# A four-layer graph network: attention over 626 node columns in place of 640, and another division of labour in the one-hot preparation

## The chip, the core and the metric

The kernel runs on one core of a Trainium2 chip. A core has a matrix engine (TensorE, PE in the profile), a vector engine (VectorE, DVE), an activation engine (ScalarE, ACT), GpSimd (POOL) and a queue for transfers (SyncE, SP). The first four compute side by side and wait for one another by semaphores; each works through its own queue in order. The metric is the time of one execution on the device, in microseconds (us).

## What is computed

Node features `x` [625, 512] go through four graph layers, each behind a layer norm and a relu, each added to `x`. There are 20,000 edges, sorted by destination.

```
h = relu(layernorm(x)); x = x + relu(mean over incoming h[src] @ W_l.T + b_l + h @ W_r.T)   # layer 0
h = relu(layernorm(x)); x = x + transformer(h)                                               # layer 1
h = relu(layernorm(x)); x = x + (sum of w(e) h[row], scaled by degrees) @ lin_w.T + lin_b    # layer 2
   w(e) = sigmoid(edge_attr_3 @ conf_w.T + conf_b)
h = relu(layernorm(x)); x = x + edge network with 64 attributes per edge                     # layer 3
# layer 1, 4 blocks: y = conditioned norm; scores = q[src] . k[dst] per head (4 heads of 128),
#   softmax over the edges of each src, out = sum of attn * v[dst]; then an MLP of 512
```

## The kernel before

Nodes lie in five tiles of 128, so 625 nodes take NP = 640 columns, and a half is HALF = 320. The program has three stages of its own: `front`, `transformer_and_gcn`, `edge_layer`; only the first two are touched.

**front** turns the edge list into two dense matrices between nodes: the count of edges, and their sum of weights. The edges are taken in 40 groups of 512 (4 tiles of 128 edges). For each tile `from_onehot` [128 edges, 640] marks the source and `to_onehot` [128 edges, 3, 64] marks the destination within a window of 64 nodes, once plain and twice multiplied by the weight's high and low part `wb`. A product on PE adds a group to PSUM, and DVE adds every second group's result into `sums` [128, 5, 3, 704], which has to be zero before. The work is divided so:

- SP loads the rows, destinations and sources first, then the attributes.
- GpSimd writes the iota (L337) and the identity (L338, L340); in the loop it multiplies `to_onehot` by the weights (L350, `weighted`).
- ScalarE fills `sums` with zeros, five instructions of 2112 elements per partition (L362), with the Exp of the weights' argument `wz` between the third and the fourth (L361). In the loop it makes the last tile of each `from_onehot` (L371, L374).
- VectorE converts the indices (L548 to L561), computes `wz` (L563 to L565), finds the windows from the rows (L569 to L581; `windows_known` lets all the engines into the loop), makes the weights (L584 to L591: plus one, reciprocal, clamp and scale, high part, back, difference, low part). Then it compares sources for groups 0 and 1 (`compare_from`, L608, three instructions per group), destinations for 0 to 3 (`compare_to`, L600), sources for 2 and 3, waits for `sums_zero`, and enters the loop. A ring of four buffers holds the groups; in the loop DVE waits for PE's group and refills.

**transformer_and_gcn** runs the four blocks. Weights and activations of the large products are split in a high and a low part, three products for one (`three`, L989). Per block: v, then q and k by feature (4 features x 2 parts, FIRST = 384 columns and REST = 256), then the attention over 20 score tiles (4 heads x 5 tiles of 128 queries). In step n PE makes the score tile n (L1068, two halves of 320 keys), turns tile n - 2 (L1076, five transposes of 128), and, from n = 8 on, makes parts of the output product of an earlier head (L1089). DVE adds the logarithm of the edge counts and takes the maximum in one instruction (L1446), ACT takes the exponential with the sum (L1267), DVE takes the reciprocal (L1453) and scales (L1456), ACT evicts the turned tile (L1273). The output is split by ACT (L1280) and DVE (L1384). A score or output product in full fp32 shows as two records each in the profile. At the head of this stage DVE takes the moments of the last tile and splits `cw` (L1392), for which PE's first product (L1017) waits. `Plan` gives each product its PSUM bank and its number on a semaphore. GpSimd splits `cw` for the coming block in mid-attention (L962) and adds row biases (L973). The second layer's matrices and the third layer use the semaphores `gcn_wt` and `gcn_lb` for their loads.

## Time and profile before

| | us |
|---|---|
| median of 3 runs | 1647.14 (1646.83 to 1648.19) |
| the profiled execution, its own time | 1645.13 |
| its span, first to last instruction | 1643.5 |
| TensorE busy | 1557.3 (95%) |
| VectorE busy | 1189.6 (72%) |
| ScalarE busy | 1102.0 (67%) |
| GpSimd busy | 677.4 (41%) |
| TensorE clock granted, mean | 0.992 |

Busy time is an average over stages. `front` takes about the first 177 us, the transformer and the second graph layer run to about 860 us, and the edge layer from there to the end. A timeline row has its start, its length, and in brackets the idle time of the engine before it, with what ended it. Short instructions on one engine can overlap by a part of their length, so starts, not lengths, tell the pace. The records of TensorE overlap too.

### The profile page before, as it was taken

To read this page: it belongs to the slowest core of one execution; us is meant where nothing else is said; L and a number is where in the kernel's file an instruction comes from. 1 tells how busy PE (TensorE), PEld (TensorE's weight loads), DVE (VectorE), ACT (ScalarE), POOL (GpSimd) and SP (SyncE) were. 2 spreads that over 40 slices of the span, in tenths; PEclk is the share of its full clock that TensorE was granted. 3 is DMA by queue.
4 is the path that set the end of the run, shared out by engine and by line. 5 is a ranking of instruction groups with operands and counts; after the bars stand their busy time and mean duration, and the time that the engine had idled before them with its cause. 6 is when DMAs were issued, how large, how long until landed. Compare 5 with 4: busy or idle time off the path is not lost. (4 is left out here: it accounts for less than half of the span.)

```text
span 1643.5 us, 24989 instructions
## 1 busy us (share of the span) xinstructions
PE 1557.3 (95%) x8530; PEld 1218.5 (74%) x8530; DVE 1189.6 (72%) x1896; ACT 1102.0 (67%) x1534; POOL 677.4 (41%) x498
## 2 busy tenths in 40 slices
PE   5889899999999999999999999999999999999987
PEld 4765586888788778877854777777777777777874
DVE  8977656556465646475723599888898888889877
ACT  9841545544554546454530699999999999999963
POOL 3410200120012001200302788788888888888601
PEclk9999899999999999999999999999999999999989
DMA  3001320012012200212007867777777777777710
GB/s 106 0 20 66 96 78 27 28 58 87 22 33 84 77 1 33 84 33 90 28 3 232 160 142 151 144 149 147 145 150 145 150 147 148 146 148 149 172 39 32
DMA packets 107046, 153.94 MB, mean 94 GB/s; under 512 B 42042, under 2 KB 47034, under 8 KB 106466
## 3 DMA queue, kind: packets, MB, share of 16 engines
q0 software_dynamic: 72832, 87.84, 28.1%
q1 hardware_dynamic: 34146, 65.21, 12.5%
q8 instruction: 41, 0.67, 0.2%
q14 instruction: 27, 0.22, 0.0%
HBM read 141.02 MB, written 11.73 MB: 93 GB/s over the span
## 5 line engine op out<-in xcount | busy, mean ns | idle before, releaser
L1772 POOL DMA_INDIRECT edge_gathered<-dst_table,edge_index x158 | 266.4, 1686 | 58.7 <-issue 53.6
L223 PE MATMUL edge_z2p<-edge_w_hi,edge_h_hi 128*128 128x512 f32 x628 | 256.6, 409 | 1.7 <-DVE edge_late L2095 1.7
L223 PE MATMUL edge_z2p<-edge_w_hi,edge_h_lo 128*128 128x512 f32 x628 | 248.6, 396 | 0.0
L223 PE MATMUL edge_z2p<-edge_w_lo,edge_h_hi 128*128 128x512 f32 x628 | 248.3, 395 | 0.0
L1741 POOL DMA_INDIRECT edge_gathered<-src_table,edge_index x158 | 201.6, 1276 | 85.4 <-POOL edge_index L1735 30.6
L973 POOL TENSOR_TENSOR h<-h,tr_row_b 128x512 f32<-128x512 f32 x40 | 59.2, 1513 | 274.2 <-ACT C L1213 273.8
L962 POOL TENSOR_TENSOR tr_cw<-w_c,tr_cw 32x1024 fp32r<-32x1024 f32 x7 | 16.6, 2376 | 346.1 <-ACT tr_cw L1173 346.1
L223 PEld LDWEIGHTS edge_z2p<-edge_w_hi,edge_h_hi 128*128 128x128 f32 x628 | 117.9, 188 | 54.9 <-issue 29.8
L223 PEld LDWEIGHTS edge_z2p<-edge_w_hi,edge_h_lo 128*128 128x128 f32 x628 | 118.1, 188 | 28.7
L223 PEld LDWEIGHTS edge_z2p<-edge_w_lo,edge_h_hi 128*128 128x128 f32 x628 | 118.1, 188 | 24.7
L2095 DVE TENSOR_TENSOR edge_late<-edge_z2p,w_c 128x1024 f32<-128x1024 f32 x79 | 96.7, 1224 | 44.9 <-PE edge_z2p L223 44.6
L989 PE MATMUL tr_one<-tr_yT_hi,tr_w_hi 128*128 128x256 f32 (+1 forms) x384 | 118.8, 309 | 4.3 <-issue 4.3
L989 PE MATMUL tr_one<-tr_yT_hi,tr_w_lo 128*128 128x256 f32 (+1 forms) x384 | 117.8, 307 | 0.0
L989 PE MATMUL tr_one<-tr_yT_lo,tr_w_hi 128*128 128x256 f32 (+1 forms) x384 | 117.8, 307 | 0.0
L2112 DVE SCALAR_TENSOR_TENSOR edge_early<-edge_early,edge_z1p 128x1024 f32<-128x1024 f32 x79 | 96.1, 1217 | 27.8 <-ACT edge_early L1981 27.8
L1267 ACT ACTIVATE hT<-hT,tr_nmax 128x640 f32<-128x640 f32 x56 | 46.3, 828 | 95.8 <-DVE tr_nmax L1446 95.4
L1977 ACT ACTIVATE edge_early<-edge_early 128x1024 f32<-128x1024 f32 x79 | 83.9, 1062 | 27.1 <-DVE edge_early L2069 27.0
L1068 PE MATMUL tr_two<-tr_kT,tr_qT 128*128 128x320 f32 x320 | 99.9, 439 | 0.1
L2123 DVE TENSOR_TENSOR edge_h_lo<-edge_early,edge_h_hi 128x1024 fp32r<-128x1024 f32 x79 | 96.8, 1225 | 2.7
L2076 DVE SCALAR_TENSOR_TENSOR edge_late<-edge_late 128x1024 f32<-128x1024 f32 x79 | 95.8, 1212 | 0.3 <-ACT edge_late L1990 0.3
L1446 DVE CUSTOM_DVE_ANT_0 hT<-tr_two,logc 128x640 f32<-128x640 f32 x80 | 65.8, 822 | 37.0 <-PE tr_two L1068 35.7
L1987 ACT ACTIVATE edge_late<-edge_late 128x1024 f32<-128x1024 f32 x79 | 82.8, 1048 | 9.6 <-DVE edge_late L2095 8.1
(364 smaller groups left out, 4019.9 us busy)
## 6 DMA issues: line engine op xcount, KB each, us to landing
w_c<-in_attr_T SPq DMA_DIRECT2D x78, 128.0 KB, 4.1
agg<-edge_sum_rows POOLq DMA_DIRECT2D x36, 128.0 KB, 10.6
w_a<-in_wv SPq DMA_DIRECT2D x4, 1024.0 KB, 5.3
w_b<-in_wq SPq DMA_DIRECT2D x4, 1024.0 KB, 5.5
w_a<-in_wk SPq DMA_DIRECT2D x4, 1024.0 KB, 7.8
w_b<-in_wo SPq DMA_DIRECT2D x4, 1024.0 KB, 7.1
w_a<-in_m SPq DMA_DIRECT2D x4, 1024.0 KB, 5.4
w_b<-in_m SPq DMA_DIRECT2D x4, 1024.0 KB, 5.3
```

The costliest lines, as they stand in the source:

```text
L223: mm = pe.matmul(out, a, b, start=(n == 0), stop=(n == last))
L989: mm = pe.matmul(out, a, b, start=(start and n == 0), stop=(stop and n == len(terms) - 1))
L1068: mm = pe.matmul(bank[:, f, 0:HALF], qT[:, h, i * P:(i + 1) * P], kT[:, h, f * HALF:(f + 1) * HALF], start=True, stop=True)
L1446: ins = dve.tensor_tensor_reduce(out=cols(scores[n % 2], HALF), in0=bank[:, :, 0:HALF], in1=cols(k.logc[:, i, :], HALF), scale=-1.0, scala ...
L1741: pool.indirect_dma_start(out=from_rows[a][:, j, :].bitcast(F32), out_offset=None, in_=k.src_table, in_offset=bass.IndirectOffsetOnAxis(ap ...
L1772: pool.indirect_dma_start(out=from_rows[ring][:, j, :].bitcast(F32), out_offset=None, in_=k.dst_table, in_offset=bass.IndirectOffsetOnAxis ...
L1977: act.activation(m1[one], m1[one], ACT.Square).then_inc(S["inner1_ready"], 1)
L1987: act.activation(m2[two], z2[two], ACT.Exp).then_inc(S["e2_ready"], 1)
L2076: dve.scalar_tensor_tensor(h2[new], m2[new], 0.5, z2[new], ALU.subtract, ALU.mult).then_inc(S["h2_ready"], 1)
L2095: dve.tensor_tensor(cols(z2[two], D), cols(ps_z2[:, :], D), b2[:, None, :].to_broadcast([P, PT, D]), ALU.add).then_inc(S["z2_ready"], 1)
L2112: dve.scalar_tensor_tensor(m1[one], m1[one], 0.5, ps_z1[one][:, :], ALU.subtract, ALU.mult).then_inc(S["h1_ready"], 1)
L2123: dve.tensor_tensor(h1_lo[one][:, :, :], cols(m1[one], EDGE), h1_hi[one][:, :, :].bitcast(F32), ALU.subtract).then_inc(S["lo_ready"], 1)
```

## The change

Attention: queries stay 5 tiles of 128, but keys and output columns end at USED = 626, in two parts of PART_A = 313. The products for q and k take 370 and 256 columns (QK_HALVES) in place of 384 and 256; the MLP keeps 384 and 256. L1446, the exponential, the scaling and the split of the output work on 626 or 313 columns. The last tile of an output product has 114 rows. Columns 626 to 640 of `qT` and of `probs_more` are filled with zeros once, by DVE at the head of the stage, and PE waits for that ahead of its first score tile. Transposes and their evictions keep 640 columns.

Preparation: GpSimd fills `sums` in place of ScalarE. ScalarE takes the Exp, and makes the reciprocal as Ln and Exp and the high part as a copy. VectorE keeps the addition of one (with a limit of 1e18 ahead of it), which now stands before the windows' table, and two instructions for the low part. Destinations are compared first. Two pairs of load semaphores become one each.

```diff
+LARGE = 1.0e18
...
@@ block.gpsimd, front @@
+                for i in range(NT):
+                    pool.memset(sums[:, i, :, :], 0.0).then_inc(sums_zero, 1)
                 n = sweeps(pool)
...
@@ block.scalar, front @@
-                act.wait_ge(ident_made, 1)
-                for i in range(NT):
-                    if i == 3:
-                        act.wait_ge(z_ready, 1)
-                        act.activation(wz[:, :], wz[:, :], ACT.Exp, scale=-1.0).then_inc(exp_ready, 1)
-                    act.activation(sums[:, i, :, :].rearrange("p a b -> p (a b)"), k.ident[:, 0:1].to_broadcast([P, 3 * WIDE]),
-                                   ACT.Copy, scale=0.0).then_inc(sums_zero, 1)
+                act.wait_ge(z_ready, 1)
+                act.activation(wz[:, :], wz[:, :], ACT.Exp, scale=-1.0).then_inc(exp_ready, 1)
+                act.wait_ge(z_ready, 2)
+                own(act.activation(wr[:, :], wz[:, :], ACT.Ln))
+                own.wait()
+                own(act.activation(wr[:, :], wr[:, :], ACT.Exp, scale=-1.0))
+                own.wait()
+                act.activation(wb[:, :, 0], wr[:, :], ACT.Copy, scale=SCALE_HI).then_inc(exp_ready, 1)
...
@@ block.vector, front @@
+                dve.wait_ge(exp_ready, 1)
+                dve.tensor_scalar(wz[:, :], wz[:, :], LARGE, 1.0, ALU.min, ALU.add).then_inc(z_ready, 1)
                 for w in range(MAXSWEEPS):
...
-                dve.wait_ge(exp_ready, 1)
-                step(dve.tensor_scalar(wz[:, :], wz[:, :], 1.0, None, ALU.add))
-                step(dve.reciprocal(wr[:, :], wz[:, :]))
-                step(dve.tensor_scalar(wr[:, :], wr[:, :], 0.0, SCALE_HI, ALU.max, ALU.mult))
-                step(dve.tensor_copy(wb[:, :, 0], wr[:, :]))
-                step(dve.tensor_copy(wf[:, :], wb[:, :, 0]))
-                step(dve.tensor_tensor(wr[:, :], wr[:, :], wf[:, :], ALU.subtract))
+                dve.wait_ge(exp_ready, 2)
+                step(dve.scalar_tensor_tensor(wr[:, :], wr[:, :], SCALE_HI, wb[:, :, 0], ALU.mult, ALU.subtract))
                 step(dve.tensor_scalar(wb[:, :, 1], wr[:, :], SCALE_LO, None, ALU.mult))
...
@@ transformer_and_gcn @@
+PART_A = -(-NODES // 2)
+USED = 2 * PART_A
+LAST_ROWS = USED - (NT - 1) * P
+QK_HALVES = slice(0, USED - 2 * P), slice(USED - 2 * P, USED)
...
@@ block.tensor, by_feature and the scores @@
-                    n = halves[f].stop - halves[f].start
+                    at = halves[f] if name == "m1" else QK_HALVES[f]
+                    n = at.stop - at.start
...
-                                mm = pe.matmul(bank[:, f, 0:HALF], qT[:, h, i * P:(i + 1) * P],
-                                               kT[:, h, f * HALF:(f + 1) * HALF], start=True, stop=True)
+                                mm = pe.matmul(bank[:, f, 0:PART_A], qT[:, h, i * P:(i + 1) * P],
+                                               kT[:, h, f * PART_A:(f + 1) * PART_A], start=True, stop=True)
...
@@ block.vector, transformer @@
+                own(dve.memset(qT[:, :, USED:NP], 0.0))
+                own(dve.memset(probs_more[:, USED:NP], 0.0))
+                own.wait()
+                dve.sem_inc(pads_ready, 1)
```

In the order of instructions the change shows at two places, the head of `front` and the attention. VectorE in `front`, before: from the last cast of the windows to the end of the weights (`wz` is 1 + exp, `wr` the weight, `wb` its two parts, `wf` the high part converted back).

```order
L581 CAST sweeps<-front_span 1x1
L584 TENSOR_SCALAR front_wz<-front_wz 128x160
L585 RECIPROCAL front_wr<-front_wz 128x160
L587 TENSOR_SCALAR front_wr<-front_wr 128x160
L588 CAST front_wb<-front_wr 128x160
L589 CAST front_wf<-front_wb 128x160
L590 TENSOR_TENSOR front_wr<-front_wr,front_wf 128x160
L591 TENSOR_SCALAR front_wb<-front_wr 128x160
```

And before, what follows: the sources of groups 0 and 1 (`w_c` is buffer 0 of `from_onehot`), two register loads (`sweeps` and `starts`), and the destinations.

```order
L608 TENSOR_SCALAR w_c<-front_iota,front_src_f 128x640 x3
L608 TENSOR_SCALAR front_from_onehot<-front_iota,front_src_f 128x640 x3
L310 TENSOR_LOAD sweeps
L310 ISA x2
L594 TENSOR_LOAD starts
L594 ISA x2
L600 ISA
L600 TENSOR_TENSOR front_to_onehot<-front_iota,front_dst 128x4x64 x2
```

VectorE in the changed kernel, from the cast of the starts on:

```order
L584 CAST starts<-front_wtab 1x440
L585 CAST sweeps<-front_span 1x1
L588 SCALAR_TENSOR_TENSOR front_wr<-front_wr,front_wb 128x160
L589 TENSOR_SCALAR front_wb<-front_wr 128x160
L310 TENSOR_LOAD sweeps
L310 ISA x2
L592 TENSOR_LOAD starts
L592 ISA x2
L598 ISA
L598 TENSOR_TENSOR front_to_onehot<-front_iota,front_dst 128x4x64 x2
L606 TENSOR_SCALAR w_c<-front_iota,front_src_f 128x640 x3
L606 TENSOR_SCALAR front_from_onehot<-front_iota,front_src_f 128x640 x3
```

Five instructions of the weights are gone, and the two register loads stand between the weights and the first destinations, ahead of the sources.

ScalarE at the start of `front`, before (`front_away` is the distance from which the last source tile is made):

```order
L355 ACT_TABLE_LOAD
L362 ACTIVATE front_sums<-ident 128x2112 x3
L361 ACTIVATE front_wz<-front_wz 128x160
L362 ACTIVATE front_sums<-ident 128x2112 x2
L371 ACTIVATE front_away<-front_iota,front_src_neg 128x640
L374 ACTIVATE w_c<-front_away 128x640
```

The same place in the changed kernel:

```order
L357 ACT_TABLE_LOAD
L360 ACTIVATE front_wz<-front_wz 128x160
L362 ACTIVATE front_wr<-front_wz 128x160
L364 ACTIVATE front_wr<-front_wr 128x160
L366 ACTIVATE front_wb<-front_wr 128x160
L374 ACTIVATE front_away<-front_iota,front_src_neg 128x640
L377 ACTIVATE w_c<-front_away 128x640
```

The five fills of `front_sums` are gone, and three activations on the weights are new. GpSimd in the changed kernel, from the iota on:

```order
L337 IOTA front_iota_i 128x704
L338 MEMSET ident 128x128
L340 AFFINE_SELECT ident<-ident 128x128
L343 MEMSET front_sums 128x2112 x5
L310 TENSOR_LOAD sweeps
L310 ISA x2
```

The five fills stand behind the identity and ahead of the load that lets GpSimd into its loop; before, that load stood directly behind the identity.

TensorE in the attention of the first block, from the first step with output products on, before:

```order
L1068 MATMUL tr_two<-tr_kT,tr_qT 128x320 x2
L1076 MATMUL tr_two<-ident,hT 128x128 x5
L1089 MATMUL tr_one<-tr_probsT,tr_v 128x320 x2
L1068 MATMUL tr_two<-tr_kT,tr_qT 128x320 x2
L1076 MATMUL tr_two<-ident,hT 128x128 x5
L1089 MATMUL tr_one<-tr_probsT,tr_v 128x320 x2
```

And in the changed kernel:

```order
L1072 MATMUL tr_two<-tr_kT,tr_qT 128x313 x2
L1080 MATMUL tr_two<-ident,hT 128x128 x5
L1094 MATMUL tr_one<-tr_probsT,tr_v 128x313 x2
L1072 MATMUL tr_two<-tr_kT,tr_qT 128x313 x2
L1080 MATMUL tr_two<-ident,hT 128x128 x5
L1094 MATMUL tr_one<-tr_probsT,tr_v 128x313 x2
```

The order is the same; score and output products have 313 columns, transposes 128 as before.

## Rows read from the trace of the kernel before

**Rows 1.** Table by stages, core 0, columns in its first line.

```profile
core 0: us, PE busy (x) PEld busy (x) DVE busy (x) ACT busy (x) POOL busy (x), PEclk, DMA share, GB/s
0.00:23.00 23.00, 6.71 (x53) 6.27 (x54) 17.90 (x57) 20.49 (x24) 5.85 (x12) 1.00 0.63 189
232.00:296.00 64.00, 60.91 (x280) 43.60 (x279) 37.69 (x92) 36.19 (x73) 2.35 (x1) 1.00 0.08 25
```

**Rows 2.** Timeline, first 23 us: start us, us, engine, line, operation.

```profile
2.38 5.67 ACT L362 ACTIVATE front_sums<-ident 128x2112 f32<-128x2112 f32 x3 [0.16 <-POOL ident L340]
...
3.24 0.42 DVE L548 CAST front_rows_f<-front_rows_i 40x512 f32<-40x512 int32 x1 [1.58 <-DMA front_rows_i<-in_dst_rows]
...
5.11 0.53 DVE L554 CAST front_iota<-front_iota_i 128x704 f16<-128x704 int32 x1
...
5.98 0.24 DVE L559 CAST front_dst<-dst_f 128x160 f16<-128x160 f32 x1
...
7.17 0.43 DVE L565 SCALAR_TENSOR_TENSOR front_wz<-front_attr,front_confb,front_wz 128x160 f32<-128x160 f32 x1
...
7.95 0.32 ACT L361 ACTIVATE front_wz<-front_wz 128x160 f32<-128x160 f32 x1
...
9.92 0.22 DVE L584 TENSOR_SCALAR front_wz<-front_wz 128x160 f32<-128x160 f32 x1
...
12.57 0.26 DVE L591 TENSOR_SCALAR front_wb<-front_wr 128x160 f16<-128x160 f32 x1
...
12.87 0.98 DVE L608 TENSOR_SCALAR w_c<-front_iota,front_src_f 128x640 f16<-128x640 f16 x3
...
14.65 0.75 DVE L600 TENSOR_TENSOR front_to_onehot<-front_iota,front_dst 128x256 f16<-128x256 f16 x2
...
16.71 3.38 PE L491 MATMUL front_sum_ps<-front_to_onehot,w_c 128*128 128x192 f16 x20 [11.12 <-POOL front_to_onehot L350]
...
22.75 0.76 DVE L600 TENSOR_TENSOR front_to_onehot<-front_iota,front_dst 128x256 f16 x2 [1.48 <-PE front_sum_ps L491]
```

**Rows 3.** Timeline of PE, the products for q, first block.

```profile
204.97 0.34 PE L989 MATMUL tr_one<-tr_yT_hi,tr_w_hi 128*128 128x384 f32 x1
...
212.25 0.28 PE L989 MATMUL tr_one<-tr_yT_hi,tr_w_hi 128*128 128x256 f32 x1
...
217.58 0.28 PE L989 MATMUL tr_one<-tr_yT_hi,tr_w_lo 128*128 128x256 f32 x1
```

**Rows 4.** Timeline of PE, output products; L1446's waits (us, times).

```profile
289.99 5.54 PE L1089 MATMUL tr_one<-C,tr_v 128*128 128x320 f32 x20
...
  PE tr_two L1068: 35.7, 48
```

**Rows 5.** Timeline of PE, head of the transformer.

```profile
180.00 1.22 PE L1017 MATMUL tr_two<-tr_cw,condT 96*128 96x512 f32 x2 [7.45 <-DVE tr_cw L1392]
```

**Rows 6.** Timeline, GpSimd beside VectorE, at 15 to 18 and 251 to 257.

```profile
15.43 1.04 POOL L350 TENSOR_TENSOR front_to_onehot<-front_to_onehot,front_wb 128x512 f16<-128x512 f16 x1 [13.08 <-DVE front_to_onehot L600]
...
15.71 1.04 DVE L600 TENSOR_TENSOR front_to_onehot<-front_iota,front_dst 128x256 f16<-128x256 f16 x1 [0.30 <-issue]
...
17.85 1.16 DVE L608 TENSOR_SCALAR front_from_onehot<-front_iota,front_src_f 128x640 f16<-128x640 f16 x1
...
251.52 0.61 DVE L1456 TENSOR_SCALAR tr_probs_more<-tr_probs_more,tr_den,has 128x640 f32<-128x640 f32 x1
...
254.03 2.35 POOL L962 TENSOR_TENSOR tr_cw<-w_c,tr_cw 32x1024 fp32r<-32x1024 f32 x1 [54.75 <-ACT tr_cw L1173]
...
254.22 2.52 DVE L1456 TENSOR_SCALAR hT<-hT,tr_den,has 128x640 f32<-128x640 f32 x1
```

**Rows 7.** Groups of GpSimd instructions: its fills (busy us, mean ns, idle).

```profile
L1726 POOL MEMSET edge_attr_w_rest<- 64x512 f32 x1 | 0.5, 519 | 0.1
...
L338 POOL MEMSET ident<- 128x128 f32 x1 | 0.2, 194 | 0.0
```

**Rows 8.** Line L628: durations, ns, minimum, median, maximum.

```profile
L628 DVE TENSOR_TENSOR front_sums<-front_sums,front_sum_ps x20: 1139/1144/1155, 23.4 to 103.8; 128x960 f32 x20
```

More of the change, by code:

```diff
@@ L612, in _ @@
                 dve.wait_ge(inputs_ready, 3)
-                for a in range(SHARE):
-                    compare_from(a, a)
                 n = sweeps(dve)
@@ L619, in _ @@
                         compare_to(a + b, a + b, start)
-                for a in range(SHARE, RING):
-                    compare_from(a, a)
+                    for b in range(SHARE):
+                        compare_from(a + b, a + b)
                 dve.wait_ge(sums_zero, NT)
@@ L1063, in _ @@
                             bank = plan.open(pe, ("S", b, n))
+                            if (b, n) == (0, 0):
+                                pe.wait_ge(pads_ready, 1)
                             if i == 0:
```

53 lines of the change are left out of this document (28 added, 25 removed).

## The prediction

> **What bounds the kernel now.** I read the table by stages first, since the shares of the whole span are a mean over different limits. In 232 to 296 us, the attention of the first block, PE is busy 60.91 of 64.00 us; in the first 23 us it is busy 6.71 and DVE 17.90 [rows 1]. So the attention edit is costed in TensorE columns, and the edit to the preparation along the chain that leads to the first one-hot product. That chain stands in the timeline [rows 2]: DVE converts the indices, finds the windows (over at 9.9), makes the weights (9.92 to 12.83), compares sources (12.87), compares destinations (14.65); GpSimd multiplies by the weights; PE's first product starts at 16.71, having idled 11.12 us for GpSimd's L350. VectorE's next round starts at 22.75, after 1.48 us of waiting for PE's second group.
>
> **Attention, what goes.** The products for q and k on the first part take 370 columns in place of 384. PE's 384-column rows start 0.1733 us apart (204.97 to 212.25, 42 steps), the 256-column rows 0.1134 (212.25 to 217.58, 47 steps) [rows 3]: 0.468 ns per column. 14 columns are 6.5 ns; there are 4 blocks x 2 products x 4 features x 12 = 384 of them: 2.5 us. Scores and output products go from 320 to 313 columns. Each is two records; 20 records of 320 columns take 5.54 us, less the last one's tail of 0.43: 5.11 / 19 = 0.269 us each [rows 4]. Seven columns of 320 are 5.9 ns; 640 records (320 of L1068, 320 of L1089) give 3.8 us. Where the step is set by DVE and not PE (DVE waits for the score product 48 times of 80, so 32 score tiles are not PE's [rows 4]) the gain comes from DVE's own 14 columns, about 15 ns in the reduction and 7 to 15 ns in the scaling, about the same as the 23 ns that PE saves per score tile. Transposes and their evictions keep 640 columns. Attention: **-6.3 us**, between -5.3 (a third of the score part lost, and 5.8 ns for q and k) and -6.9.
>
> **Attention, what comes.** Two small fills by DVE stand at the head of the transformer, ahead of the moments and of the split at L1392, for which PE waits there (7.45 us of idle, [rows 5]). 56 and 14 elements per partition, each bounded by L584's 160 elements in 0.22 us [rows 2], with one more wait: **+0.25 us** (0.1 to 0.5). The wait for pads_ready is ahead of the first score product, some 50 us later: nothing. The merged load semaphores wait for loads that were due long before: nothing.
>
> **Preparation, the straight count.** ScalarE no longer fills sums (3 fills in 5.67 us and two more [rows 2]), so Exp can start when z is ready, and Ln, Exp and the copy (0.32 us each, as L361) are over while DVE writes the windows. Of DVE's 2.91 us from 9.92 to 12.83 there remain one operation like L565 (0.43) and L591 (0.26); one of about 0.24 moves ahead of the windows. The weights would be ready at 9.99 + 0.25 + 0.75 = 11.0 instead of 12.83. But the sources' comparisons no longer lie over the two register loads: with a load idle of 0.30 [rows 6], 0.6 us is exposed. Then 0.75 for two destination comparisons and 0.98 for the first sources' group, in which two operations must now wait for GpSimd's products (1.04 us for one, [rows 6]; with restarts 2.1). PE starts at 11.0 + 0.6 + 0.75 + 0.98 + 2.1 = 15.4, not 16.71: **-1.3 us**, and DVE's next round, whose own queue then ends about when PE's second group does, moves with it. From there the period is DVE's, as before, so the shift is kept.
>
> **Preparation, the fills on GpSimd.** That count takes DVE's early operations at their present price. GpSimd's fills: 128 elements 0.194 us, 512 elements 0.519 [rows 7], so 0.846 ns per element, and 2112 elements are 1.87 us, five 9.4 us, from 2.38 on, where ScalarE's first fill starts now behind the same identity [rows 2]. In the same time DVE runs L548, L554, L556, L558 and L559, the last three 0.24 us each. Does a fill hold them up? The trace shows a product by GpSimd doing so: L962 runs 254.03 to 256.38, and DVE's scaling, begun at 254.22, takes 2.52 us where the same work at 251.52 takes 0.61 [rows 6]. It also shows the manner: with GpSimd's L350 issued one behind the other, DVE's L600 at 15.71 takes 1.04 us and L608 at 17.85 takes 1.16, though 0.75 and 0.98 are the sums for two and three of them alone [rows 2, 6]. They take turns, one and one. These GpSimd instructions read and write; the fills only write, and no row has a fill beside a DVE cast. So the price is bounded from nothing to a full turn for each of five fills. I take the full turn, since the nearest rows are full blocks and not slowdowns.
> The Trainium skill (SBUF — State Buffer, section Who interferes with whom) has a rule for it: a DVE cast, copy or tensor_scalar in a 2-port mode and a GpSimd instruction exclude each other for the whole instruction. L554's 704 elements in 0.53 us are more than one per cycle of 0.96 GHz (the page VectorE: DVE Perf Modes, Specifications), so by that rule it would be such a cast. By the rule the sum is the one of the next paragraph, without it the one above.
>
> Turn by turn: fill 1 2.38 to 4.25; L548 (ready at 3.24) 4.25 to 4.67; fill 2 to 6.54; the two reductions run beside it; L554 6.54 to 7.07; fill 3 to 8.94; L556 to 9.18; fill 4 to 11.05; L558 to 11.29; fill 5 to 13.16; L559 at 13.16, where it is at 5.98 now. That is +7.2 us on everything behind. PE's first product then comes at 15.4 + 7.2 = 22.6 against 16.71: **+5.9 us** for the preparation, between +4.5 (one turn fewer) and +7.2 (DVE waits until all five are done, at 11.7, with its first cast: 8.5 - 1.3).
>
> **Sum.** -6.3 + 0.25 + 5.9 = -0.15 us. On the profiled execution's 1645.13 that is 1645.0; the median of the runs is 2.0 higher, 1647.14, so the forecast is **1647 us**. Its own range, from the ends above: -6.9 + 0.1 + 4.5 = -2.3 to -5.3 + 0.5 + 7.2 = +2.4, so 1644.8 to 1649.5.
>
> **Rivals.**
> 1. *The fills hold nothing up.* For it: they read nothing, and no row shows a fill blocking a cast. Against it: in [rows 6] the block lasts the whole instruction, which looks like a resource held and not one shared. -6.3 + 0.25 - 1.3 = -7.35: 1639.8 us.
> 2. *Odd rows are dearer (slower).* The score reduction L1446 now works on two rows of 313 elements, the second of which starts on an odd word. If that row ran at half rate, each tile would cost 0.33 us more; on the 32 tiles that are DVE's, 10 us, and with the forecast's preparation 1657. It turns the change to slower from about 0.11 us per tile on (3.5 us over 32). Against it: L628 adds windows that start at any column and takes 1139 to 1155 ns in all 20 cases [rows 8].
> 3. *The narrower products save nothing* (PE's time set by something other than columns). Then -6.3 goes: 1653.3. The 384 and 256 column steps speak against it [rows 3].
> A sub-case of the forecast, DVE getting no turn until the last fill (+7.2 for the preparation), gives 1648.3.
>
> **Chances.** Forecast 0.55 and its late sub-case 0.05; rival 1 0.28; rival 2 0.08; rival 3 0.04. Something over 0.2% (3.3 us) is what a measurement of this kernel can tell from no change. Faster by that (under 1643.8): rival 1 and 0.05 of the forecast's case if a turn or two is skipped, 0.33. Slower (over 1650.4): rivals 2 and 3, 0.12. Same: 0.55. The range goes from a little below rival 1 to the forecast's upper end, 1638.8 to 1649.6, and leaves the slower cases and the tails out.
>
> **What would show it.** In the changed kernel: five GpSimd fills of 1.87 us; L551 (rows cast) with 1.4 us or so instead of 0.42, L557, L559 and L560 near 2 us each, and PE's first one-hot product near 22.6 (forecast) or 15.4 (rival 1). ACT's four small operations before DVE's L588. In attention: L1094's 20 records in 5.43 us, q and k steps of 0.1668 us, L1446's counterpart at 0.81 us. The forecast is wrong if the early casts keep their present times beside the fills, or if the span from the first score tile to the end of the fourth block shrinks by much less than 6 us.

## The result, and the profile after

| | before | changed |
|---|---|---|
| median of 11 runs each, on one chip | 1647.60 us (1645.71 to 1649.46) | 1653.20 us (1650.62 to 1659.89) |
| ratio, 95% interval | | 1.0035 (1.0026 to 1.0044) |
| the profiled execution | 1645.13 us | 1654.87 us |
| its span | 1643.5 us | 1653.2 us |

The change makes the kernel about 6 us slower (4 to 7 us by the interval). Here and below the ratio stands with its interval, and is not the quotient of the two medians beside it: the two differ by up to 0.0007, which is 1.2 us. The time of 1653.2 lies above the range, which ended at 1649.6.

The beginning, timeline of the changed kernel (start us, us, engine, line, operation, and in brackets the idle time before and what ended it). L551 is what was L548, L589 was L591, L598 was L600, L494 was L491:

```profile
2.29 9.05 POOL L343 MEMSET front_sums<- 128x2112 f32 x5
3.00 8.62 DVE L551 CAST front_rows_f<-front_rows_i 40x512 f32<-40x512 int32 x1 [1.34 <-DMA front_rows_i<-in_dst_rows]
...
13.07 0.53 DVE L557 CAST front_iota<-front_iota_i 128x704 f16<-128x704 int32 x1
...
15.58 0.34 ACT L360 ACTIVATE front_wz<-front_wz 128x160 f32<-128x160 f32 x1 [13.36 <-DVE front_wz L567]
...
18.41 0.26 DVE L589 TENSOR_SCALAR front_wb<-front_wr 128x160 f16<-128x160 f32 x1
20.32 0.76 DVE L598 TENSOR_TENSOR front_to_onehot<-front_iota,front_dst 128x256 f16<-128x256 f16 x2 [1.65 <-issue]
...
23.68 3.38 PE L494 MATMUL front_sum_ps<-front_to_onehot,w_c 128*128 128x192 f16 x20 [10.13 <-DVE w_c L606]
...
30.03 0.76 DVE L598 TENSOR_TENSOR front_to_onehot<-front_iota,front_dst 128x256 f16 x2 [1.59 <-PE front_sum_ps L494]
```

The first cast took 0.42 us in [rows 2]. Here it is open for 8.62, and ends 0.3 us behind the last of the five fills. The reduction behind it starts at 11.65 instead of 3.69, so VectorE is 8.0 us late from there on, and TensorE's first one-hot product comes at 23.68 against 16.71. Behind the weights stand 1.65 us in which VectorE computes nothing: the two register loads.

The products for k of the first block: first and last of the 48 with 370 columns, then of the 48 with 256:

```profile
225.73 0.34 PE L990 MATMUL tr_one<-tr_yT_hi,tr_w_hi 128*128 128x370 f32 x1
...
233.88 0.34 PE L990 MATMUL tr_one<-tr_yT_hi,tr_w_lo 128*128 128x370 f32 x1
234.05 0.28 PE L990 MATMUL tr_one<-tr_yT_hi,tr_w_hi 128*128 128x256 f32 x1
...
239.69 0.28 PE L990 MATMUL tr_one<-tr_yT_hi,tr_w_lo 128*128 128x256 f32 x1
```

8.15 / 47 = 173.4 ns for 370 columns, where 384 took 173.3 [rows 3], and 5.64 / 47 = 120.0 ns for 256 columns that start at column 370, where the same count from column 384 took 113.4 [rows 3].

Output products, and the score reduction (durations in ns, minimum, median, maximum; then its waits):

```profile
297.64 5.43 PE L1094 MATMUL tr_one<-C,tr_v 128*128 128x313 f32 x20
...
L1458 DVE CUSTOM_DVE_ANT_0 hT<-tr_two,logc x80: 797/810/814, 241.2 to 762.6; 128x626 f32<-128x626 f32 x80
...
  PE tr_two L1072: 34.9, 48
```

The output products take 5.43 us instead of 5.54 [rows 4]. The reduction had this line before, and now takes 15 ns less:

```profile
L1446 DVE CUSTOM_DVE_ANT_0 hT<-tr_two,logc x80: 810/825/826, 232.9 to 756.0; 128x640 f32<-128x640 f32 x80
```

All the kernels below issue the same 8530 products in the same order, so the start of one product can be compared from trace to trace. The table gives by how many us a product starts later than in the profile of before. The columns beside the changed kernel are runs of the next section; "again" is one more profile of the kernel before, and shows how far two executions of one program lie apart: up to 1.3 us.

| product, start before | changed | again | prep_only | attn_only | fills_act | qk_384 | best | prep_act_only |
|---|---|---|---|---|---|---|---|---|
| first one-hot, 16.7 | +6.96 | +0.05 | +5.25 | -0.17 | -0.68 | +6.96 | -0.69 | -0.68 |
| one-hot, 103.1 | +7.27 | -0.90 | +4.55 | -1.14 | -1.24 | +6.65 | -1.74 | -0.84 |
| first of the transformer, 180.0 | +7.61 | -0.90 | +4.56 | -0.81 | -0.91 | +6.91 | -1.44 | -0.54 |
| first for q, 203.8 | +7.60 | +0.22 | +4.21 | +0.13 | +0.23 | +6.65 | -0.49 | -0.77 |
| first score, 231.5 | +8.36 | +0.21 | +4.20 | +0.88 | +0.98 | +6.72 | -0.50 | -0.77 |
| last output, block 1, 295.1 | +7.55 | +0.20 | +4.20 | +0.08 | +0.18 | +5.94 | -1.31 | -0.78 |
| last output, block 4, 770.6 | +6.42 | +0.75 | +4.55 | -0.75 | -0.84 | +3.92 | -4.28 | -0.86 |
| 810.4 | +8.00 | +0.82 | +6.16 | +0.84 | +0.80 | +5.54 | -2.70 | -0.80 |
| 1635.0 | +9.74 | +1.28 | +6.61 | +1.07 | +1.05 | +5.64 | -2.82 | +1.12 |

A part of the first rows is such a difference and not an edit. The kernel's old `front` stands in three profiles (before, again, attn_only), and by 103.1 they lie at 0, -0.90 and -1.14 us. Most of it comes from TensorE's second group of 20 products, which lasts 2.45 us in before and 1.65 in the other two, at a granted clock of 1.00 in all of them. VectorE's next round waits for that group; in before it starts at 22.75 after 1.48 us of waiting [rows 2], in again at:

```profile
21.84 0.76 DVE L600 TENSOR_TENSOR front_to_onehot<-front_iota,front_dst 128x256 f16 x2 [0.53 <-PE front_sum_ps L491]
```

So the +7.27 of the changed kernel and the small gains of the others at 103.1 are known to about 1 us. Four of the early ones (again, attn_only, fills_act, best) also lose 0.9 to 1.1 us between 180.0 and 203.8, where the clock is low in every profile (over 176 to 205 us a mean of 0.76 or 0.77 in these four and 0.78 in before).

In the changed kernel the attention itself (first score to last output) gains 0.81, 0.78, 0.80 and 0.86 us in the four blocks; from the first product for q to the first score it loses 0.75, 0.68, 0.50 and 0.01. The two last steps, +1.6 by 810 and +1.7 at the end, are the clock. Two windows of the changed kernel, and then the windows of before in which the same work runs (the granted clock is the first number after the engines):

```profile
806.00:815.00 9.00, 7.00 (x36) 5.94 (x35) 5.70 (x7) 2.52 (x6) 3.80 (x3) 0.81 0.32 102
1600.00:1612.00 12.00, 9.39 (x34) 7.28 (x34) 6.19 (x12) 1.10 (x2) 0.00 (x0) 0.50 0.01 1
```

```profile
798.00:807.00 9.00, 6.83 (x48) 6.17 (x48) 7.29 (x8) 3.51 (x9) 5.40 (x4) 1.00 0.13 28
1592.00:1604.00 12.00, 9.39 (x37) 7.23 (x37) 6.21 (x12) 1.10 (x2) 0.00 (x0) 0.59 0.00 1
```

The first is 0.19 x 9 = 1.7 us of clock. Near the end both profiles have a stretch at the lower level (0.50 of full speed), and it is longer in the changed kernel: 0.50 over its 12 us and 0.94 over the 8 us behind them, against 0.59 and 1.00 before, 1.6 us together. prep_act_only has the longer stretch too, without the fills on GpSimd and without the new attention. So the 9.7 us between the two profiles are 6.4 us of the change and 3.3 us of clock, and the ratio says 0.0035 x 1647 = 5.8.

### The profile page after: what moved, and what is told of

Its sections match the earlier page's. It is cut to its first block and busy times, and to the rows that moved or that the text cites. A ratio compares the mean times of both kernels' runs of the same rounds, so it can differ in the third digit from the quotient of the medians.

```text
span 1653.2 us, 24993 instructions
## 1 busy us (share of the span) xinstructions
PE 1559.7 (94%) x8530; PEld 1223.5 (74%) x8530; DVE 1187.5 (72%) x1894; ACT 1091.5 (66%) x1532; POOL 684.6 (41%) x503
## 5 line engine op out<-in xcount | busy, mean ns | idle before, releaser
L1784 POOL DMA_INDIRECT edge_gathered<-dst_table,edge_index x158 | 261.6, 1656 | 59.3 <-issue 54.5
L1753 POOL DMA_INDIRECT edge_gathered<-src_table,edge_index x158 | 185.3, 1173 | 85.7 <-issue 35.7
L224 PEld LDWEIGHTS edge_z2p<-edge_w_hi,edge_h_hi 128*128 128x128 f32 x628 | 117.9, 188 | 54.9 <-issue 29.8
L990 PE MATMUL tr_one<-tr_yT_hi,tr_w_hi 128*128 128x256 f32 (+2 forms) x384 | 119.6, 312 | 4.3 <-issue 4.3
L990 PE MATMUL tr_one<-tr_yT_lo,tr_w_hi 128*128 128x256 f32 (+2 forms) x384 | 118.7, 309 | 0.0
L990 PE MATMUL tr_one<-tr_yT_hi,tr_w_lo 128*128 128x256 f32 (+2 forms) x384 | 118.7, 309 | 0.0
L1274 ACT ACTIVATE hT<-hT,tr_nmax 128x626 f32<-128x626 f32 x56 | 45.7, 817 | 95.4 <-DVE tr_nmax L1458 94.6
L1072 PE MATMUL tr_two<-tr_kT,tr_qT 128*128 128x313 f32 x320 | 98.3, 433 | 0.1
L1458 DVE CUSTOM_DVE_ANT_0 hT<-tr_two,logc 128x626 f32<-128x626 f32 x80 | 64.6, 807 | 36.2 <-PE tr_two L1072 34.9
```

Of the source, the lines that this page charges most:

```text
L224: mm = pe.matmul(out, a, b, start=(n == 0), stop=(n == last))
L990: mm = pe.matmul(out, a, b, start=(start and n == 0), stop=(stop and n == len(terms) - 1))
L1072: mm = pe.matmul(bank[:, f, 0:PART_A], qT[:, h, i * P:(i + 1) * P], kT[:, h, f * PART_A:(f + 1) * PART_A], start=True, stop=True)
L1753: pool.indirect_dma_start(out=from_rows[a][:, j, :].bitcast(F32), out_offset=None, in_=k.src_table, in_offset=bass.IndirectOffsetOnAxis(ap ...
L1784: pool.indirect_dma_start(out=from_rows[ring][:, j, :].bitcast(F32), out_offset=None, in_=k.dst_table, in_offset=bass.IndirectOffsetOnAxis ...
```

## The experiments

**Each part alone.** prep_only has the changed `front` and the old transformer, attn_only the reverse.

> The preparation of the changed kernel, with the attention of the kernel before. In the changed kernel five GpSimd fills of 1.81 us stand back to back and DVE's first cast, begun at 3.00, ends at 11.62; PE's first one-hot product is 6.96 us later and DVE's next round 7.28 us later. Theory A (the fills hold out DVE's casts and the delay is kept to the end): the span is 7.3 us longer than before, 0.44% of 1647: ratio 1.0044, and the first cast shows the same 8.6 us. Theory B (the attention part is what costs, the preparation's delay is absorbed by waits behind it): ratio 1.000 to 1.002. Rival C (the loss depends on something else of the whole kernel, such as the clock in the late edge stage): the front shows +7 us but the end something other than +7.3 by more than 1 us.

Measured: 1653.35 us against 1646.74, ratio 1.0047 (1.0033 to 1.0061). The preparation alone is the whole loss. The ratio gives 7.7 us (5.4 to 10.0) and the medians 6.6; the table has +4.55 up to the end of the fourth block and +6.61 at 1635. Its profile is not a copy of the changed kernel's beginning, though the code is:

```profile
3.05 3.17 DVE L551 CAST front_rows_f<-front_rows_i 40x512 f32<-40x512 int32 x1 [1.39 <-DMA front_rows_i<-in_dst_rows]
6.26 0.68 DVE L552 TENSOR_REDUCE front_lo_span<-front_rows_f 40x1 f32<-40x512 f32 x1
...
7.67 0.73 DVE L557 CAST front_iota<-front_iota_i 128x704 f16<-128x704 int32 x1
8.32 1.97 DVE L559 CAST front_src_f<-src_i 128x160 f32<-128x160 int32 x1
10.21 1.97 DVE L560 CAST dst_f<-front_dst_i 128x160 f32<-128x160 int32 x1
12.22 0.24 DVE L561 CAST front_dst<-dst_f 128x160 f16<-128x160 f32 x1
```

The durations of its five fills (minimum, median, maximum), and those of the changed kernel:

```profile
L343 POOL MEMSET front_sums<- x5: 1853/1945/2227, 2.3 to 10.1; 128x2112 f32 x5
```

```profile
L343 POOL MEMSET front_sums<- x5: 1852/1852/1852, 2.3 to 9.5; 128x2112 f32 x5
```

In prep_only the casts come in between the fills: the first is open for 3.17 us, until about the end of the second fill, and two later ones for 1.97 each, about one fill; the reduction keeps its 0.68 us beside a fill. In the changed kernel no cast comes in. Both happen with the same instructions: of the eight profiles with five back-to-back fills, five show no turn (one of them two_operands, with its one instruction of the kind) and three show turns. Either way the fills are over at 11 to 12 us, but with turns a part of the casts is done by then: the first one-hot product is 5.25 us late and not 6.96. Why an execution goes one way or the other stays open.

> The attention of the changed kernel, with the preparation of the kernel before. From the two traces: pads at the head +0.33; scores and output products -0.9 per block, -3.6 in all; q and k +0.6 per block, +2.4. Theory A (these three add up): -0.9 us, ratio 0.9995, no difference that a measurement can tell. Theory B (as predicted: q and k gain 2.5 us, and what the trace of the changed kernel shows there comes from the shifted start of the stage): -6.0 us, ratio 0.9964. Rival C (the lower clock seen late in the changed kernel comes from its denser attention): +2 to +3 us, ratio 1.001 to 1.002.

Measured: 1645.39 against 1646.74, ratio 0.9996 (0.9986 to 1.0005). Theory A's -0.9 us (0.9995) lies in that interval, and the -6.0 of the prediction (0.9964) far outside it.

**The fills back on ScalarE** (fills_act), the rest of the new preparation kept:

```diff
-                for i in range(NT):
-                    pool.memset(sums[:, i, :, :], 0.0).then_inc(sums_zero, 1)
...
+                for i in range(3):
+                    fill(i)
                 act.wait_ge(z_ready, 1)
                 act.activation(wz[:, :], wz[:, :], ACT.Exp, scale=-1.0).then_inc(exp_ready, 1)
...
                 act.activation(wb[:, :, 0], wr[:, :], ACT.Copy, scale=SCALE_HI).then_inc(exp_ready, 1)
+                for i in range(3, NT):
+                    fill(i)
```

> The changed kernel with the five fills back on ScalarE (three ahead of the weights' activations, two behind), the rest of the new preparation kept: weights by ScalarE, destinations first. Theory A (the fills on GpSimd are the whole loss of the preparation): DVE's casts take 0.42, 0.53 and 0.24 us again, PE's first one-hot product comes at 15.4 to 16.5 us, and against the changed kernel 7.5 to 8.5 us go: about 1645 where the changed kernel takes 1653, ratio to before 0.9985 to 0.9995. Theory B (the new order of the comparisons or the weights on ScalarE cost by themselves): PE's first product stays behind 17.5 us, and the ratio to before is over 1.001.

Measured: 1645.72 against 1646.74, ratio 0.9992 (0.9981 to 1.0002). The first cast takes 0.42 us again, and the first one-hot product starts at:

```profile
10.77 0.26 DVE L595 TENSOR_SCALAR front_wb<-front_wr 128x160 f16<-128x160 f32 x1
12.68 0.76 DVE L604 TENSOR_TENSOR front_to_onehot<-front_iota,front_dst 128x256 f16<-128x256 f16 x2 [1.65 <-issue]
...
16.03 3.38 PE L500 MATMUL front_sum_ps<-front_to_onehot,w_c 128*128 128x192 f16 x20 [10.47 <-DVE w_c L612]
```

Against the changed kernel's 23.68 that is 7.65 us for the fills alone; against 16.71 before it is -0.68 for all the rest of the new preparation. That is theory A.

**A gap between the fills** (fills_wait): `pool.wait_ge(sums_zero, i + 1)` behind each.

> The changed kernel with a wait between the fills on GpSimd: each waits for the one before it to be complete (about 0.16 us, as between the identity's two instructions). In two profiles of the changed front the five fills took 9.05 us and DVE's first cast 8.36 to 8.62 us; in a third the fills took 9.79 us, and three casts took 3.17, 1.97 and 1.97 us between them. Theory A (the way is held from instruction to instruction while the next fill follows without a gap, and a gap hands it to DVE): the first cast ends behind the first fill, at 4.2 to 4.6, then one cast per fill; the fills end at 12 to 13 us. Theory B (a gap makes no difference, GpSimd takes precedence): the first cast ends only with the fifth fill, at about 12.2. Either way the first one-hot product stays 5 to 7 us behind that of before, 22 to 24 us.

```profile
3.27 1.16 DVE L552 CAST front_rows_f<-front_rows_i 40x512 f32<-40x512 int32 x1 [1.60 <-DMA front_rows_i<-in_dst_rows]
...
5.87 0.73 DVE L558 CAST front_iota<-front_iota_i 128x704 f16<-128x704 int32 x1
6.52 1.97 DVE L560 CAST front_src_f<-src_i 128x160 f32<-128x160 int32 x1
8.41 1.99 DVE L561 CAST dst_f<-front_dst_i 128x160 f32<-128x160 int32 x1
10.44 1.88 DVE L562 CAST front_dst<-dst_f 128x160 f16<-128x160 f32 x1
```

Now the first cast ends at 4.43, with the first fill, and one cast passes per fill: theory A. One profile shows it, and turns occurred in some profiles without a gap too. The first one-hot product is at 21.82 (I had expected 22 to 24), better than 23.68, the same as the 21.96 of the profiles with turns, and still 5.1 us behind that of before: a gap shares the time out but does not remove the price.

**The other kind of instruction** (two_operands): the fills as changed, six early VectorE instructions with two tensor operands.

```diff
-                step(dve.tensor_copy(rows_f[:, :], rows_i[:, :]))
+                step(dve.tensor_tensor(rows_f[:, :], rows_i[:, :], rows_i[:, :], ALU.max))
```

and so for the other casts; the negation became `scalar_tensor_tensor(src_f, -2.0, src_f, mult, add)`.

> The changed kernel, fills on GpSimd, but VectorE's six early instructions that read one tensor (the casts of the rows, the iota, the sources, the destinations twice, and the negation of the sources) are written with two tensor operands: the maximum of a tensor with itself, and -2x + x. They give the same values. In all profiles so far the reductions and the two-operand instructions beside a fill kept their price, while casts waited for the end of one fill or of all five. Theory A (what the fills hold out is a kind of VectorE instruction, the cast and tensor_scalar): none of the six waits, the cast of the rows takes 0.5 to 0.7 us, and the arguments of the weights, where one tensor_scalar is left, are reached near 6.5 us; that one waits for at most one fill if turns are given, up to the last fill's end (11.3) if not. Theory B (the fills hold out every VectorE instruction that comes to its start while one runs): the first of the six takes 8.4 us again.

```profile
2.30 9.05 POOL L343 MEMSET front_sums<- 128x2112 f32 x5
```

```profile
2.93 0.68 DVE L551 TENSOR_TENSOR front_rows_f<-front_rows_i 40x512 f32<-40x512 int32 x1 [1.27 <-DMA front_rows_i<-in_dst_rows]
...
5.07 0.89 DVE L557 TENSOR_TENSOR front_iota<-front_iota_i 128x704 f16<-128x704 int32 x1
5.88 0.32 DVE L559 TENSOR_TENSOR front_src_f<-src_i 128x160 f32<-128x160 int32 x1
...
6.71 0.32 DVE L563 SCALAR_TENSOR_TENSOR front_src_neg<-front_src_f 128x160 f32<-128x160 f32 x1
6.95 4.49 DVE L565 TENSOR_SCALAR front_wz<-front_attr,front_confb 128x160 f32<-128x160 f32 x1
```

This is the clearest picture of the cause. The same fills run underneath; all six rewritten instructions pass at 0.32 to 0.89 us, and the one tensor_scalar that is left, 0.38 us elsewhere, waits 4.49 until the fifth fill is over at 11.35. The first one-hot product comes at 20.49, 3.2 us earlier than in the changed kernel. The Trainium skill (SBUF — State Buffer, section Who interferes with whom) has both halves as a rule: casts, copies and tensor_scalar in a 2-port mode exclude GpSimd, and an instruction with two SBUF inputs contends only with a GpSimd instruction that reads. The traces agree with both: the casts are held for whole fills, and a form with two inputs passes beside fills, which read nothing, while beside GpSimd's reading L350 one comparison of this form took 1.04 us [rows 6], where two take 0.75 alone [rows 2].

**q and k split at 384 and 256 again** (qk_384), scores and output products still at 313 columns:

```diff
-QK_HALVES = slice(0, USED - 2 * P), slice(USED - 2 * P, USED)
+QK_HALVES = FIRST, REST
```

> The changed kernel with the products for q and k split at 384 and 256 columns as before, over 640 (so the pad of the queries needs no fill); scores and output products stay at 313 columns. In the run with the four splits a pair of 370 and 256 columns cost 173.1 + 120.0 = 293.1 ns, the pair before 173.3 + 113.4 = 286.7: 6.4 ns x 192 pairs = 1.2 us; and the changed kernel lost 0.31 us per product for q or k, 8 x 0.31 = 2.4 us, by the time shift of its trace. Theory A (the split costs): the step of the 256-column products is 113.4 ns again and the time from the first score tile's start to the fourth block's end as in the changed kernel; against the changed kernel 1.2 to 2.5 us less, ratio to before 1.0020 to 1.0030. Theory B (the split costs nothing, the shift was drift of the clock): the same time as the changed kernel, ratio to before 1.0035 to 1.0045.

Measured: 1649.94 against 1645.86, ratio 1.0020 (1.0011 to 1.0029), where the changed kernel has 1.0035. By these ratios the split costs about 2.5 us, by the medians 1.5, and the two intervals still overlap, so the times alone do not settle it. The traces do better. From the first product for q to the first score the blocks lose 0.07, 0.00, 0.65 and 0.00 us here instead of 0.75, 0.68, 0.50 and 0.01, and the attention keeps its -0.8 per block. Over all profiles, the seven with 384 and 256 lose between -0.4 and +1.2 us in the four blocks together (mean 0.35, before itself 0), the five with 370 and 256 lose 1.9 four times and 3.1 once. So the split costs 1.5 us or a little more. The step of the 256-column products is 113.4 ns again in the first two blocks, and 117.8 in the last two, of which more below.

**Which columns cost.** Four profiles with other splits of q and k, the first two with several sizes mixed in a block, the last two with one case per block:

> The changed kernel with the products for q and k split at another column for each of the four features: 384/242, 368/258, 360/266 and 370/256, to read the pitch of the products in one trace. Before: 384 columns from column 0 in 173.3 ns, 256 from 384 in 113.4 ns. Theory U (the moving operand is read in units of 16 columns, 64 bytes, and every unit touched counts): 384 and 370 from column 0 173 ns, 368 166 ns, 360 166 ns; 242 from 384 113 ns, 258 from 368 120 ns, 266 from 360 127 ns, 256 from 370 120 ns. Theory E (units of 8 columns): 368 166, 360 162, 370 170; 258 from 368 117, 266 from 360 120, 256 from 370 117. Theory L (columns count one by one, as predicted, and what the changed kernel shows is of another cause): 370 167, 360 162; 242 107, 258 114, 266 118, 256 from 370 113. Rival N (under 256 columns the product falls to a slower rate): 242 takes over 200 ns.

> The changed kernel with two more sets of splits for q and k. In blocks 0 and 2 the second part always has 256 columns and starts at column 384, 376, 372 or 370, and the first part has as many columns (overlapping nothing; the second part may run past 626). In blocks 1 and 3 the first part is 384 columns and the second starts at 384 with 256, 248, 244 or 242 columns. Measured so far: 384 from 0 173.3 ns, 370 173.1, 368 168.6, 360 165.5; 256 from 384 113.4, 242 from 384 114.4, 258 from 368 120.5, 266 from 360 124.0, 256 from 370 120.0. Theory S (the start decides: a start off a multiple of 64 bytes or 16 columns costs one more unit): 256 columns from 376, 372 and 370 all about 120 ns, and 248, 244 and 242 from 384 all 113 to 115 ns. Theory C (the count decides: counts that are not multiples of 8 or so are slow): 256 from 376 and 372 113 ns as from 384, 248 from 384 110 ns, and 244 and 242 more than 113.

> The changed kernel with one split of q and k per block: block 1 384 columns, and 256 from column 370 (14 columns are written twice); block 2 384, and 242 from 384; block 3 370, and 256 from 370, as changed; block 4 384, and 256 from 384, as before. Theory S (the start off 384 costs): the second part takes 120 ns in blocks 1 and 3, 113 to 114 in 2 and 4 (or 118 where that level occurs). Theory C (the count of the first part costs the second too): block 1 113 to 118, block 3 120. Theory L (columns one by one): 242 columns take 107 ns, 370 take 167.

> The same with block 1 384 columns, and 256 from 376; block 2 384, and 256 from 371; block 3 384, and 258 from 368; block 4 370, and 256 from 384 (leaving out columns 370 to 383 of q and k there). Theory U (a start within a unit of 16 columns costs the rest of the unit): 256 from 376 and from 371 both 120 ns, 258 from 368 120 ns. Theory P (what counts is a start on an odd column or off a multiple of 8): 376 gives 113, 371 over 120. For block 4: 173 ns for the 370 columns if units are read whole, 167 if columns count one by one.

The fourth block of parts_b leaves columns 370 to 383 of q and k unmade, so it serves for the steps alone. Three second parts of parts_a, first and last of 48 each: 256 columns from 370, 242 from 384, and 256 from 384.

```profile
218.53 0.28 PE L995 MATMUL tr_one<-tr_yT_hi,tr_w_hi 128*128 128x256 f32 x1
...
224.29 0.29 PE L995 MATMUL tr_one<-tr_yT_hi,tr_w_lo 128*128 128x256 f32 x1
```

```profile
378.85 0.27 PE L995 MATMUL tr_one<-tr_yT_hi,tr_w_hi 128*128 128x242 f32 x1
...
384.18 0.28 PE L995 MATMUL tr_one<-tr_yT_hi,tr_w_lo 128*128 128x242 f32 x1
```

```profile
709.42 0.28 PE L995 MATMUL tr_one<-tr_yT_hi,tr_w_hi 128*128 128x256 f32 x1
...
714.96 0.28 PE L995 MATMUL tr_one<-tr_yT_hi,tr_w_lo 128*128 128x256 f32 x1
```

They are 122.6, 113.3 and 117.8 ns. Steps of all the splits, each the mean over a run of 11 or 47 (first parts of q in whose run other waits or a change of level fall are left out):

| part | ns |
|---|---|
| 384 from 0 | 173.3 to 174.7, in other runs of products 176.5 to 176.7 |
| 370 from 0 | 173.0 to 173.4, or 170.0 |
| 376, 372, 368, 360 from 0 | 170.3 to 172.6, 169.5 to 170.0, 168.6, 165.5 |
| 256 from 384 | 113.4 to 115.2, or 117.6 to 118.3 |
| 248, 244, 242 from 384 | 113.2, 114.2, 113.3 to 114.4 |
| 256 from 370 | 120.0 to 122.7 |
| 256 from 376, 372, 371 | 117.4 to 118.7, 118.9, 116.6 to 116.8 |
| 258 from 368 | 120.5 to 122.0 |
| 266 from 360 | 124.0 |

Two things are settled. A count below 256 buys nothing (242 takes what 256 takes, where columns one by one would give 107), and below 384 the first 14 columns buy 0 to 3.3 ns instead of 6.5. And the start alone costs: behind unchanged 384 columns, 256 from 370 take 122.6 ns. What is not settled is the rule. Theory U (units of 16 columns) fits 370, 360 and 256 from 370, and fails on 368 (166 expected, 168.6 measured), on 266 from 360 (127 expected, 124.0 measured) and on 256 from 371 (120 expected, 116.7); theory P (a start off a multiple of 8) fails on 376 (113 expected, 117.4 to 118.7), theory C on the cost of the start alone. And the same product has two levels, 113.4 and 117.8 ns (173.3 and 176.7), which hold for a whole run of 48 and change from run to run without any edit: the fourth block of the kernel before is at the upper level, which is why the split seems to cost nothing there. What sets the level stays open, and it blurs the comparison of single rows by 4 ns. The fourth block of parts_b has both levels beside each other, 370 columns at 170.0 ns with 256 from 384 at 113.7, and 370 at 173.0 with 117.9; if the levels of the two parts go together, as this one block suggests, the 14 columns buy 3.3 ns at either level, half of the forecast.

**The best of both** (best): fills on ScalarE, q and k at 384 and 256, scores and output products at 313, and of the pads only the one of `probs_more`, filled behind `cb_scaled` instead of ahead of the moments.

> What the runs leave as worth keeping: the fills on ScalarE with the new preparation around them (first one-hot product 16.03 against 16.71, DVE's next round 21.50 against 22.75), q and k at 384 and 256 columns, scores and output products at 313, and the one pad that is left filled by DVE behind the scaling of cb and not at the head of the stage. Sum against before: -1.25 - 3.6 + 0 = -4.9 us, ratio 0.9970. Theory A (the terms add up): 0.9965 to 0.9975. Theory B (the preparation's gain is lost by the end of the edge groups, since the loop's pace is another engine's): -3.6, ratio 0.9978. Rival C (scores and output products save nothing that lasts to the end): 0.9992.

Measured: 1643.39 against 1645.86, ratio 0.9982 (0.9972 to 0.9992): faster than both kernels, but 3.0 us by the ratio (1.3 to 4.6 by its interval), where the terms gave 4.9. The table has -4.28 at the end of the fourth block, and then +1.6 by 810 us, a spell of lower clock that the profile of before does not have.

**The order of the comparisons, and the preparation without fills.** order_old is best with the sources of groups 0 and 1 first again; prep_act_only is fills_act's preparation with the old attention.

> The run called best, with the sources of groups 0 and 1 compared first again, as before the change. In best 1.65 us lie open between the weights (11.03) and the first destinations (12.67), for two register loads. Working it out from best's rows: sources 11.1 to 12.9, destinations from 12.9, GpSimd's product from 13.7, first one-hot product of TensorE at 14.9 instead of 16.02; VectorE's next round, whose queue is 1.77 us earlier than before's 22.75, at 21.0, as best's 21.02. Theory A (the loop's pace is VectorE's, so the earlier first product is waited away): same time as best, ratio to before 0.997 to 0.9985. Theory B (the new order costs the 1.1 us for good): 1 us less than best, ratio 0.9965 to 0.9975.

> The new preparation with the fills on ScalarE, and the attention of the kernel before. It takes the run called best (0.9982 of before) apart: what is left is the preparation without its fills. The profiles have VectorE's next round at 21.50 or 21.02 against 22.75, so 1.25 to 1.7 us by the rows. Theory A (kept to the end): ratio 0.9990 to 0.9993, and with the 3.6 us of the scores and output products the 1643.4 of best would be 1.5 us too long, which then is the clock at the head of the transformer. Theory B (given back by 110 us or at the head of the transformer): 0.9996 to 1.0002.

order_old: 1643.37 against 1647.30, ratio 0.9973 (0.9964 to 0.9982); beside best's 0.9982 the intervals overlap, and its own times have the same median as best's. In its profile the loads lie under work again and the first product is at 15.13, but VectorE then waits for TensorE's groups:

```profile
21.68 0.76 DVE L604 TENSOR_TENSOR front_to_onehot<-front_iota,front_dst 128x256 f16 x2 [2.44 <-PE front_sum_ps L500]
```

Best's round begins at 21.02, after 0.23 us of waiting. So the 0.9 us of the earlier first product is gone by then, and the order makes no difference that I could measure. That is theory A's time, but its reason is not shown: TensorE's second group lasts 2.96 us in this profile and 1.65 in best's, and in the two profiles of the unedited kernel it lasts 2.45 and 1.65, so the wait may belong to the execution and not to the order. prep_act_only: 1646.80 against 1647.30, ratio 1.0004 (0.9993 to 1.0016). Its column is -0.54 to -0.86 from the first product to 810 us, so the new preparation without its fills gains about 0.7 us by the rows, below what the times can show; my theory A (0.9990 to 0.9993) asked for twice that. Only the first product shows this gain clear of the differences between executions (-0.68 or -0.69 in three profiles, against +0.05 and -0.17 in again and attn_only).

**The kernel before once more.**

> The kernel before, unchanged, for one more profile. In six profiles of variants TensorE's granted clock over 795 to 820 us was 0.93, in that of before 1.00, which is 1.5 us of the difference between two profiles. Theory A (the dip comes and goes with the execution): this profile has 0.93 there too, or another spot at a lower clock, and the span is 1643.5 to 1646. Theory B (the dip belongs to the edit): 1.00 again at 795 to 820 us.

```profile
795.00:820.00 25.00, 22.84 (x126) 19.90 (x125) 18.67 (x29) 13.60 (x34) 9.22 (x6) 1.00 0.13 43
```

1.00 again, which was theory B's number. But over all sixteen profiles of this study that window has 0.93 in eight and 1.00 in the other eight, and both occur with the old attention (prep_only 0.93, prep_act_only 1.00) and with the changed one (attn_only 0.93, order_old 1.00), with fills on ScalarE and on GpSimd (qk_384 0.93, fills_wait 1.00). So it goes with no part of the edit: a dip worth about 1.6 us that some profiles have, and the two profiles compared first happened to lie on either side of it. It has no fixed place either: order_old, with 1.00 in that window, loses 1.7 us between 140 and 160 us, where its granted clock is 0.83 over 150 to 160.

## Why the prediction was wrong, point by point

**Attention, scores and output products: right.** -3.8 forecast; 0.81 + 0.78 + 0.80 + 0.86 = 3.25 us gained in the trace, with the same per block in attn_only, qk_384 and best. The cover by VectorE held: its waits for score tiles stayed at 48.

**Attention, q and k: the step that failed most.** I drew a line through two sizes, 256 and 384 columns [rows 3], took 0.468 ns per column from it, and applied that to 370. Both sizes and both starts (0 and 384) are round; the edit's are not, and it moved the start of the second part along with the count of the first, which the sum did not mention at all. Forecast -2.5; measured about +2 (0.75 + 0.68 + 0.50 + 0.01 = 1.9 against the trace of before, 1.6 against the mean of all seven profiles with the old split, 2.5 by the ratios). That is about 4.4 of the 6.4 us by which the sum missed. I had the rival "narrower products save nothing" at 0.04, for all the products at once, with "the 384 and 256 column steps speak against it". They did not speak about 370. For the fp32 scores, which show as two records of 313 columns each, it was false, and for the three-term products true.

**The pads: right.** +0.25 forecast, 7.27 to 7.61 = +0.34 measured, +0.33 in attn_only and fills_act, +0.26 with one of the two pads in qk_384. But best and prep_act_only, which have no pad there, show +0.30 as well, since the split L1392 then waits 0.33 us for ScalarE; so taking the pads away from the head gained nothing in best.

**The preparation: mechanism right, size short.** That the fills exclude VectorE's casts for whole instructions, and leave reductions alone, is what the runs show. Forecast +5.9 at the first one-hot product, measured +6.96 there and +7.28 at VectorE's next round, which the table shows kept. Two terms were off. The turns: I took one and one from [rows 6], where GpSimd's products alternate with VectorE, and gave the late sub-case (no turn until the last fill) 0.05; it is what five of eight profiles show. The sub-case's own +7.2 for the preparation lies near the +6.96 partly by luck: it is 8.5 of delay less 1.3 for the rest, and the runs show 8.0 of delay on VectorE and 0.68 for the rest. And the exposed register loads: 0.6 us forecast, from an idle of 0.30; measured 1.65 (two register loads with no work running over them). With 1.05 us more there the straight count of -1.3 would be -0.25; fills_act shows -0.68 at the first product, so the rest of that count was 0.4 us too dear.

**The sum** was forecast as -6.3 + 0.25 + 5.9 = -0.15. With what was measured it is 1.9 - 3.25 + 0.34 + 7.27 = +6.3, and the ratio gives +5.8. **Odd rows** (rival 2) did not exist: 810 ns for 626 elements, 825 for 640. **The range**: it was cut at the forecast's upper end, and the two rivals above it were dropped, each small alone. Its own row of bounds for q and k (-2.5 to -2.2) had no end at zero or above, though no row of the trace had such a start or count.

## What to carry to other kernels

Before fills (or any work) go to an idle GpSimd, list the VectorE instructions that run beside them by kind: casts and tensor_scalar wait for whole GpSimd instructions, reductions and two-operand forms pass beside a fill. ScalarE did the same fills at no price that a run shows. And a width that is cut from a round number is not cheaper by its share of the columns: price a count and a start by rows with such a count and start, and where there are none, let the bound reach zero and past it.

## What was not expected of the hardware

- Five GpSimd fills of 1.852 us in a row let a waiting VectorE cast in between in three profiles and not at all in five. One and the same cast of 0.42 us was open for 3.17 us in one profile and for 8.62 in another, with the same instructions around it.
- A three-term product of 256 columns takes 113.4 ns from column 384 and 120.0 to 122.7 from column 370; 242 columns take as long as 256. Full fp32 output products went from 320 to 313 columns at their share (5.54 to 5.43 us for 20 records).
- The same run of products has two levels, 113.4 and 117.8 ns, without any edit; over a block's q and k that is 48 x (4.4 + 3.4) ns x 2 = 0.75 us, where the traces have 0.61 to 0.66 between a block at one level and at the other.
- Two register loads with no work above them cost VectorE 1.65 us of idle time, the same to 0.01 in the profiles of the changed kernel, fills_act and fills_wait.
